# Layer norms and the queries' normalisation with the tokens on partitions: variances, roots and inverses on 112x16 tiles, spread back by transposes

## What is computed

```python
def _layernorm(x, axis=-1, eps=1e-05):
    m = jnp.mean(x, axis=axis, keepdims=True)
    v = jnp.var(x, axis=axis, keepdims=True)
    return (x - m) / jnp.sqrt(v + eps)

def _l2norm(x, eps=1e-12):
    n = jnp.sqrt(jnp.sum(x * x, axis=-1, keepdims=True))
    return x / jnp.maximum(n, eps)

x = x + jnp.tanh(g_xattn[0]) * _L0_xattn_ref(_layernorm(x), ctx_768, ctx_768, ...)
x = x + jnp.tanh(g_ffn[0]) * _L0_ffn_ref(_layernorm(x), ...)
# ... the same for layers 1, 2 and 3
```

## Time and profile before

| | before |
|---|---|
| median of 3 runs | 4428.92 us |
| profiled execution | 4428.97 us |
| its span | 4427.3 us |
| TensorE matmul busy | 3752.2 us (85%) |
| VectorE busy | 2734.5 us (62%) |
| ScalarE busy | 2056.9 us (46%) |
| GpSimd busy | 1422.6 us (32%) |

### The profile page before, as it was taken

One profiled execution on the slowest core, in us unless ns is written; L12 is line 12 of the kernel. 1 busy time (PEld: TensorE's weight loads), 2 busy tenths in 40 slices (PEclk: granted clock), 3 DMA queues, 4 the chain that ended last, 5 costly groups with the idle time before them and its releaser, 6 DMA issues. The chain is left out here.

```text
span 4427.3 us, 85895 instructions
## 1 busy us (share of the span) xinstructions
PE 3752.2 (85%) x33246; PEld 2490.9 (56%) x33246; DVE 2734.5 (62%) x3533; ACT 2056.9 (46%) x2955; POOL 1422.6 (32%) x1888
## 2 busy tenths in 40 slices
PE   7389999945379999998999997679867799989996
PEld 7267777723236666664666664257523366656663
DVE  8656666552255555525555553467554899989993
ACT  7167777711113334332433442166412477767762
POOL 0164545213422323212333220022101655656630
PEclk9689999967779999997999997889988799999997
DMA  6166767544232223212332320021000666666640
GB/s 170 47 149 162 172 165 171 127 157 176 68 73 73 82 81 86 77 45 72 86 88 77 85 76 24 9 64 47 5 17 20 149 156 152 149 140 152 155 105 15
DMA packets 197059, 434.56 MB, mean 98 GB/s; under 512 B 45707, under 2 KB 98877, under 8 KB 196588
## 3 DMA queue, kind: packets, MB, share of 16 engines
q1 hardware_dynamic: 122308, 339.44, 29.1%
q0 software_dynamic: 38912, 47.06, 5.0%
q10 hardware_dynamic: 35504, 43.39, 3.7%
HBM read 244.72 MB, written 32.67 MB: 63 GB/s over the span
## 5 line engine op out<-in xcount | busy, mean ns | idle before, releaser
L1471 DVE TENSOR_REDUCE L_mp<-ps 112x2 f32<-112x1000 f32 x384 | 458.2, 1198 | 508.1 <-PE ps L1293 504.6
L1330 PE MATMUL ps<-L_p,L_cn 125*97 125x448 f32 x1536 | 639.2, 538 | 0.0
L1454 ACT ACTIVATE L_p<-ps 125x896 f32<-125x896 f32 x384 | 352.2, 917 | 613.7 <-PE ps L1318 540.5
L2141 ACT ACTIVATE L_p<-L_p 125x896 f32<-125x896 f32 x384 | 364.7, 950 | 228.7 <-DVE L_p L2194 228.0
L2177 DVE TENSOR_REDUCE L_mp<-ps 112x2 f32<-112x1000 f32 x384 | 455.6, 1191 | 6.6 <-PE ps L1954 6.6
L2194 DVE SCALAR_TENSOR_TENSOR L_p<-ps,xn 125x896 f32<-125x896 f32 x384 | 414.8, 1082 | 41.0 <-PE ps L1973 30.0
L1316 PE MATMUL ps<-L_qh,L_ch 97*125 97x448 f32 x768 | 386.0, 503 | 14.0 <-DMA L_qh<-L_mc 14.0
L1330 PEld LDWEIGHTS ps<-L_p,L_cn 125*97 125x97 f32 x1536 | 250.4, 163 | 205.9 <-issue 165.9
L1954 PE MATMUL ps<-L_ks,L_qs 96*128 96x500 bf16 x768 | 236.3, 393 | 62.4 <-DVE L_mp L2177 50.7
L918 ACT ACTIVATE L_p<-ps,rk 125x896 f32<-125x896 f32 x256 | 257.5, 1007 | 68.0 <-PE ps L775 64.2
L1317 PE MATMUL ps<-L_ql,L_ch 96*125 96x448 f32 x768 | 284.5, 370 | 0.0
(11 more groups left out here) (531 smaller groups left out, 7446.8 us busy)
## 6 DMA issues: line engine op xcount, KB each, us to landing
L_ks<-L_k_part SPq DMA_DIRECT2D x288, 375.0 KB, 7.4
L_ks<-L_k_first SPq DMA_DIRECT2D x96, 375.0 KB, 6.2
moe_w<-in_L_w SPq DMA_DIRECT2D x64, 512.0 KB
L_cn<-in_ctxN SPq DMA_DIRECT2D x32, 568.4 KB
cs_ct<-in_ctxT SPq DMA_DIRECT2D x32, 562.5 KB, 4.2
L_raw<-in_ctxT SPq DMA_DIRECT2D x32, 562.5 KB
L_cr<-in_ctxT POOLq DMA_DIRECT2D x32, 562.5 KB, 4.7
L_ch<-in_ctxT POOLq DMA_DIRECT2D x32, 562.5 KB, 4.4
```

The costliest lines, as they stand in the source:

```text
L1330: mm = nc.tensor.matmul(U[:, a, :], CN[s][:, j, :], P[:, n % 2, a * HALF:(a + 1) * HALF], start=(j == 0), stop=(j == KT - 1))
L1454: nc.scalar.activation(two(P[:, n % 2, :]), SB[n % 2], ACT.Exp).then_inc(S["exped"].sem, 1)
L1471: nc.vector.tensor_reduce(mp[:, 2 * k:2 * k + 2], ps[0:TT, bank:bank + 2, 0:500], AX.X, ALU.max).then_inc(S["chunk_maxed"].sem, 1)
L2141: nc.scalar.activation(two(P[0:KP, n % 3, :]), two(P[0:KP, n % 3, :]), ACT.Exp).then_inc(S["exped"], 1)
```

## The change

The variances of 112 tokens are made with the tile of squares as the stationary operand and one column of `J` as the moving one, so that they land as one column with the tokens on partitions. Sixteen such columns fill a 112x16 tile in bank 4. Root and reciprocal work on this tile. Sixteen transposes then take one column each, repeated 128 times, against the 112x112 identity, which puts the inverses of 112 tokens on all 128 partitions. A root of one element is put ahead of the squares on ScalarE, so that its table of functions is loaded there. In `l2_norm_queries` the sums, root, maximum and reciprocal are made in the same way, one root and one reciprocal for all chunks, and the multiplication reads the spread inverses from PSUM.

```diff
@@ layer_norm
-        sd = core.sb(f"sd{tag}", [128, CH], F32, ctx)
-        rs = core.sb(f"rs{tag}", [128, CH], F32, ctx)
+        sd = core.sb(f"sd{tag}", [TT, NT], F32, ctx)
+        rs = core.sb(f"rs{tag}", [TT, NT], F32, ctx)
+        warm = core.sb(f"warm{tag}", [1, 1], F32, ctx)
...
                 for c in range(NCH):
                     pe.wait_ge(sq.sem, sq.at(c + 1))
-                    mm = nc.tensor.matmul(ps[G * c:G * (c + 1), 4, 0:CH], core.J[:, 0:G], x2[:, columns(c)],
-                                          start=True, stop=True)
+                    for t in range(per * c, per * (c + 1)):
+                        mm = nc.tensor.matmul(ps[0:TT, 4, t:t + 1], x2[:, t * TT:(t + 1) * TT], core.J[:, 0:1],
+                                              start=True, stop=True)
                 mm.then_inc(var.sem, 1)
                 pe.wait_ge(inv.sem, inv.at(1))
                 for c in range(NCH):
-                    nc.tensor.matmul(ps[:, c, 0:CH], core.ident[:, G * c:G * c + 1].to_broadcast([128, D]),
-                                     rs[:, :], start=True, stop=True).then_inc(spread.sem, 1)
+                    for k in range(per):
+                        t = per * c + k
+                        mm = nc.tensor.transpose(ps[:, c, k * TT:(k + 1) * TT],
+                                                 rs[:, t:t + 1].to_broadcast([TT, D]), core.ident[0:TT, 0:TT])
+                    mm.then_inc(spread.sem, 1)
...
+                nc.scalar.activation(warm[:, :], core.eps[0:1, :], ACT.Sqrt)
                 for c in range(NCH):
                     act.wait_ge(cen.sem, cen.at(c + 1))
                     nc.scalar.activation(x2[:, columns(c)], xc[:, columns(c)], ACT.Square).then_inc(sq.sem, 1)
                 act.wait_ge(var.sem, var.at(1))
-                nc.scalar.activation(sd[:, :], ps[:, 4, 0:CH], ACT.Sqrt, bias=core.eps[:, :]).then_inc(std.sem, 1)
+                nc.scalar.activation(sd[:, :], ps[0:TT, 4, 0:NT], ACT.Sqrt, bias=core.eps[0:TT, :]).then_inc(std.sem, 1)
@@ l2_norm_queries
                 for c in range(NCH):
                     pe.wait_ge(sqd.sem, c + 1)
-                    nc.tensor.matmul(core.ps[:, 4 + c, 0:CH], core.ones[:, :], x2[:, c * CH:(c + 1) * CH],
-                                     start=True, stop=True).then_inc(mm2.sem, 1)
+                    for t in range(per * c, per * (c + 1)):
+                        mm = nc.tensor.matmul(core.ps[0:TT, 4, t:t + 1], x2[:, t * TT:(t + 1) * TT],
+                                              core.ones[:, 0:1], start=True, stop=True)
+                mm.then_inc(mm2.sem, 1)
+                pe.wait_ge(inverted.sem, 1)
+                for c in range(NCH):
+                    for k in range(per):
+                        t = per * c + k
+                        mm = nc.tensor.transpose(core.ps[:, c, k * TT:(k + 1) * TT],
+                                                 inv[:, t:t + 1].to_broadcast([TT, D]), core.ident[0:TT, 0:TT])
+                    mm.then_inc(spread.sem, 1)
...
-                act.wait_ge(sqd.sem, NCH)
-                for c in range(NCH):
-                    act.wait_ge(mm2.sem, c + 1)
-                    nc.scalar.activation(x2[:, c * CH:(c + 1) * CH], core.ps[:, 4 + c, 0:CH],
-                                         ACT.Sqrt).then_inc(nrm.sem, 1)
+                act.wait_ge(mm2.sem, 1)
+                nc.scalar.activation(norm[:, :], core.ps[0:TT, 4, 0:NT], ACT.Sqrt).then_inc(nrm.sem, 1)
...
+                dve.wait_ge(nrm.sem, 1)
+                link(nc.vector.tensor_scalar(norm[:, :], norm[:, :], 1e-12, None, ALU.max))
+                nc.vector.reciprocal(inv[:, :], norm[:, :]).then_inc(inverted.sem, 1)
                 for c in range(NCH):
                     s = slice(c * CH, (c + 1) * CH)
-                    dve.wait_ge(nrm.sem, c + 1)
-                    link(nc.vector.tensor_scalar(x2[:, s], x2[:, s], 1e-12, None, ALU.max))
-                    link(nc.vector.reciprocal(x2[:, s], x2[:, s]))
-                    link(nc.vector.tensor_tensor(qn[:, s], qp[:, s], x2[:, s], ALU.mult))
+                    dve.wait_ge(spread.sem, c + 1)
+                    link(nc.vector.tensor_tensor(qn[:, s], qp[:, s], core.ps[:, c, 0:CH], ALU.mult))
```

More of the change, by code:

```diff
@@ L178, in layer_norm @@
     added = core.gate_added
-    G = 128 // NCH
+    per = CH // TT
     done, core.done = core.done, []
@@ L359, in l2_norm_queries @@
     w_in = core.sig("l2q_w_in")
-    mm1, qpd, sqd, mm2, nrm = (core.sig(f"l2q_{n}") for n in ("mm", "qp", "sq", "sum", "norm"))
+    mm1, qpd, sqd, mm2, nrm, inverted, spread = (core.sig(f"l2q_{n}") for n in (
+        "mm", "qp", "sq", "sum", "norm", "inverted", "spread"))
     with ExitStack() as ctx:
@@ L363, in l2_norm_queries @@
         x2 = core.sb("l2q_x2", [D, T], F32, ctx)
+        norm = core.sb("l2q_norm", [TT, NT], F32, ctx)
+        inv = core.sb("l2q_inv", [TT, NT], F32, ctx)
+        per = CH // TT
         with nc.Block() as block:
```

## The result

The changed kernel takes 4383.28 us in the median (4381.77 to 4391.9), the kernel before 4430.07 beside it on the same chip (4426.8 to 4431.75): a ratio of 0.990, 95% interval 0.988 to 0.992, or 46.8 us less where 53.5 were forecast. The profiled execution took 4382.35 us with a span of 4380.7, which is 46.6 less than that of before, so its stages can be set beside those of before one by one.

The account below looks back on a forecast made before the run. Bound: the serial chain inside the layer norms and queries' normalisation, each alone between barriers. Saved 45.5 (eight layer norms) + 4.65 ("f3") + 10.1 (queries) - 6.7 (lower clock afterwards) = 53.5 us, from 4428.97 to 4375.5; range 4363 to 4387.

Parts of the forecast that it names:

- tails: Eight layer norms without "f3", last square to last multiplication: 5.65 us each, from 90.70 in all, 45.5 us saved.
- fold: Small products of the next attention's weights behind "a1": begin at half clock, 1.3 us lost, up to 2.9.
- queries' block: The queries' normalisation, from the last square to its end: 6.85 us instead of 16.95, 10.1 us saved.
- the case in which the clock falls early: Rival: last variance chunk of ten blocks at half clock, 7 us, with 9.9 us lost behind them; 4386, chance 0.15.
- Root, reciprocal, transposes, multiplications: Rest of a layer norm after the variance: root 0.20, reciprocal 0.25, transposes with multiplications 4.0 us, plus hand-overs.
- f3: Layer norm whose reciprocal starts only behind VectorE's binarisation: 4.3 us from there instead of 8.95, 4.65 us saved.
- the first rival: Clock stays up: transposes at full clock, 8 us more saved, nothing lost in next stages; 4361, chance 0.14.
- Variance: In a layer norm, three chunks of products hide behind the squares; the last ends 1.0 us after the last square.
- Table load: ScalarE's load moves ahead of the squares: 0.3 us gained in each of six norms, contained in the windows' sum.
- Give-back: Stages behind the changed blocks begin at half clock: 6.7 us lost, bounds 0 and 9.9.
- Logits and last feed-forward: Begin at half clock: logits behind "f1" and "f2" 6.15 us each, 4.1 us lost; last feed-forward 1.3 lost.
- a rival with the whole give-back of 9.9: Transposes never lift the clock, so the next stages lose the full 9.9 us; 4378.7, chance 0.15.

Follow-up runs that it names:

- The doubled variance: The changed kernel with every variance product of the nine norms issued two times; 4434.72 us, ratio 1.0018.
- the fp32r one: The changed kernel with squares and the column of 1/128 in the rounded float32 format, two moving columns, also in the queries' block; 4364.85 us, ratio 0.9858.
- the two fp32r kernels: The changed kernel with variance in the rounded float32 format, with the one-element root ahead of the squares (4364.85 us) and without it (4373.16 us).
- the fill: The changed kernel with three unread 448-column products more in "a1", one between variance and spread, two behind the transposes; 4382.47 us.

## Why the prediction was right or wrong

- **The frame held, the sum in part by luck.** The blocks stand alone between barriers, and what they lost came off the end. 4383.3 lies in the range, 8 us above the forecast. Behind it are two misses of 7.3 (tails) and 6.4 us (fold) on one side, and on the other 4.0 us from stages that nobody changed and 2.6 in the queries' block, 1.5 of them by the clock ahead of it. The time is near the price of the case in which the clock falls early (4386), but mostly for another reason: of the 8.3 us more in the eight waits for the variance, 6.2 are the backlog, which stands at full clock too (1.82 instead of 1.04 us), and 2.1 the clock.
- **Root, reciprocal, transposes, multiplications, "f3":** right, 4.67 in "o0" against 4.60. The rows of this size and of the sixteen transposes carried over; in "a2", "a3" and the queries' block the transposes ran mostly at full clock, as the first rival had it for all ten.
- **Variance: the step that failed first.** "The first three chunks hide behind the squares" compared 0.8 us of records with 0.75 us between squares, and left out that TensorE is on the means until some 1.4 us before the last square. About 14 records are done by then and the rest stand behind it: 1.82 to 2.56 us from last square to root instead of 1.04. The rows on hand showed this: in "o0" of the kernel before the first variance record starts at 896.93, 1.34 us before the last square ends. For the queries' block the forecast did count from when TensorE comes free, 2.0, and 1.75 was measured. The doubled variance (all 32 more records on the path) and the fp32r one (16 records, 0.64 everywhere) show it from both sides. The price of a record was right, 0.10 us at full clock. In five of the nine norms ("o0", "f0", "a1", "f1", "f3") the clock fell among the records, as the rival had it; that cost 0.2 to 0.7 us each.
- **Table load:** the 0.3 us in each of six are not there, as the variance outlasts the load. They appear, larger, once the variance is short: 4.2 us between the two fp32r kernels. There the trace shows the root directly behind a load of 1.28 us, 1.31 from the last square's end to the root. The Trainium skill ("ScalarE: Activation LUTs", What ACT_TABLE_LOAD costs) gives 2.66 us for a switch, 1.28 for the load and the rest for a drain; the trace agrees on the load, and shows no drain.
- **Give-back: the term that was mis-sized.** Logits and last feed-forward came as worked out. The fold was costed as if the clock rose after up to 5.7 us, as in the first mean, and then at half of that: 1.3 us, where 7.7 were measured. But that row was of 448-column products; from the variance of "a1" on, through the fold and the products behind it, the clock did not rise for 34 us. The products behind the fold (1.5 of the 7.7 us) were not in the forecast at all. The whole give-back was 13.0 us, beyond the forecast's upper bound of 9.9. The old layer norm in "a1" and the fill both restore 6.90 us; the run with the queries' block alone shows that the old norm doesn't always keep the clock up either.
- **The rule that transposes don't lift the clock:** in the fp32r kernel the clock rose at 1211.9 with nothing but the sixteen transposes behind it since 1208.68, and in "a3" of the changed kernel the transposes ran at full clock (sixteen in 1.88 us). The Trainium skill ("TensorE: Matmul & The Clock Gate", Part 4: PE-mode transpose) states that full clock doesn't engage for transposes; these traces don't agree with it. The forecast gave it a rival with the whole give-back of 9.9. More than that came back, but the transposes are not what decided it: with ordinary products in their place the fold still took 12.20 us.
- **Queries' block:** 10.4 in two profiles and 12.7 in a third, for a forecast of 10.1.

## What to carry to other kernels

When a step is cut into many small products, count from when the engine comes free, not from when the data come: the queue behind the earlier work is what sticks out. A long wasteful stretch of an engine can be holding up its clock for the next stage; before removing it, look whether the next stage consists of small products like the fold's, under which the clock never rose here, and take the rate for it from a row of such products at the lower clock. A hidden cost (here the table load) has to be measured again once its cover has been cut.

## What the runs showed of the hardware

- The fold's small f32 products kept the clock that they found, or lost it. Of thirteen profiles, five have the fold at 0.50 from its start, and it stays there for all 13.08 us, though TensorE doesn't pause. Eight have it start at 1.00: in five it takes 6.90 us, in three the clock falls 1 to 2 us into it (11.17 to 12.20 us). Two 448-column products right ahead of the fold were enough to keep it at 1.00.
- Transposes can be followed by a rise of the clock. Behind "f3" in the changed kernel, TensorE idled for 3.09 us, ran the sixteen transposes at half clock, and was at full clock behind them:

```profile
4337.67 3.25 PE L219 MATMUL ps<-ident,rsf 112*128 112x112 f32 x16 [3.09 <-DVE rsf L258]
...
4340.72 1.09 PE L2936 MATMUL ps<-ident,bin_w 128*128 128x128 f32 x8
```
```profile
4337.70:4340.80 3.10, 3.10 (x17) 3.10 (x18) 1.76 (x3) 0.00 (x0) 0.00 (x0) 0.50 0.00 0
4340.80:4343.00 2.20, 1.01 (x9) 0.77 (x7) 1.81 (x3) 0.00 (x0) 0.00 (x0) 0.99 0.00 0
```

- A product with one f32 column is two records of 0.10 us each at full clock (32 in 3.22 us), during nearly all of which a load of the stationary squares runs (3.13 us); at half clock the logits' records of the same stationary size take 0.19. As fp32r with two columns a product is one record, and the last four take 0.55 us.
- The experts' stage took 301.6 and 306.0 us in two executions of the changed kernel, and single runs of one kernel differ by as much as 19 (the kernel before beside the first four: 4416.97 to 4435.82), with no place for it that the profiles show. What causes this was not tried, and it is why gains of 4 us in place (the fill, the old norm in "a1") could not be told in the medians.
